# Alternating the four pages of an expert group row by row in DRAM

## What is computed

```python
def ffn(x, expert_sel, keys, values):          # 64 experts, 128 wide
    sel_val, sel_idx = top_k(sigmoid(x @ expert_sel.T), 4)
    gates = zeros.at[row, sel_idx].set(sel_val)
    h = einsum('nd,kde->nke', x, keys)
    return einsum('nke,kev->nv', relu(h) * gates[:, :, None], values)

x = x + attn_a(layernorm(x))   # causal, 16 heads of 8, rotary, W_attn, W_proj
x = x + ffn(layernorm(x), ...)
x = x + attn_b(layernorm(x))   # one head, local band of 64, softmax
x = x + ffn(layernorm(x), ...)
```

## Time and profile before

| | us |
|---|---|
| median of 3 runs | 1199.96 |
| lowest and highest run | 1194.97, 1205.8 |
| span of the profiled execution | 1216.6 |

### The profile page before, as it was taken

One profiled execution on the slowest core, in us unless ns is written; L12 is line 12 of the kernel. 1 busy time (PEld: TensorE's weight loads), 2 busy tenths in 40 slices (PEclk: granted clock), 3 DMA queues, 4 the chain that ended last, 5 costly groups with the idle time before them and its releaser, 6 DMA issues.

```text
span 1216.6 us, 22596 instructions
## 1 busy us (share of the span) xinstructions
PE 818.3 (67%) x7290; PEld 601.3 (49%) x7290; DVE 728.4 (60%) x2057; ACT 560.2 (46%) x1505; POOL 876.4 (72%) x934
## 2 busy tenths in 40 slices
PE   1899978888688766697898665454458874991000
PEld 0444444443344325697898644343357774991000
DVE  3787988888878424764667846566256772661111
ACT  1177666676566743564565413333126552661000
POOL 6345667879767675887888878878727578887776
PEclk9789999999999986898999866567679897996555
DMA  6556544533272332599898412212325564994222
GB/s 182 171 181 210 191 159 172 171 99 105 75 232 58 96 95 76 144 264 215 176 215 177 81 44 42 39 46 37 100 72 162 149 183 127 263 273 106 69 63 63
DMA packets 226258, 163.80 MB, mean 135 GB/s; under 512 B 15968, under 2 KB 213600, under 8 KB 226144
## 3 DMA queue, kind: packets, MB, share of 16 engines
q1 hardware_dynamic: 183968, 110.43, 31.7%
q0 software_dynamic: 36096, 33.59, 13.8%
q10 hardware_dynamic: 6080, 18.35, 4.1%
HBM read 78.94 MB, written 83.36 MB: 133 GB/s over the span
## 4 chain that ended last, share of the span: by engine, by line
PE 37%; POOL 23%; DVE 15%; issue 14%; ACT 6%; another core or an unknown queue 3%; DMA 3%; ACTq 0%; POOLq 0%; DVEq 0%; SPq 0%
POOL x_res L1743 7%; PE ps L771 6%; PE ps L780 5%; PE ps L672 5%; POOL sorted_rows L1727 4%; POOL v_aug L1745 3%; PE ps L631 3%; PE ps L760 3%; POOL x_scaled L1745 2%; ACT arena L978 2%; DMA x_res<-result_rows,dest 2%; DVE row_max L1211 2%; PE ps L689 2%; POOL arena L1776 1%
## 5 line engine op out<-in xcount | busy, mean ns | idle before, releaser
L1743 POOL DMA_INDIRECT x_res<-result_rows,dest x176 | 274.1, 1557 | 60.6 <-issue 48.8
L978 ACT ACTIVATE arena<-ps 128x512 f32<-128x512 f32 x320 | 182.8, 599 | 79.9 <-PE ps L604 75.1
L1727 POOL DMA_INDIRECT sorted_rows<-v_aug,dest x144 | 139.7, 970 | 83.7 <-issue 33.8
L1410 DVE COPY arena<-ps 128x512 f32<-128x512 f32 x128 | 88.2, 689 | 132.0 <-PE ps L760 71.7
L771 PE MATMUL ps<-arena 128*128 128x128 f32 x1024 | 147.2, 290 | 23.0 <-DVE arena L1410 11.5
L631 PE MATMUL ps<-arena 64*128 64x128 bf16 (+3 forms) x576 | 130.2, 305 | 28.9 <-DMA arena<-k_parts 15.1
L771 PEld LDWEIGHTS ps<-arena 128*128 128x128 f32 x1024 | 134.4, 205 | 26.9 <-issue 13.9
L1211 DVE TENSOR_REDUCE row_max<-ps 128x1 f32<-128x512 f32 (+1 forms) x192 | 127.0, 682 | 33.6 <-PE ps L651 31.9
L967 ACT COPY arena<-ps 128x512 f32<-128x512 f32 x128 | 75.0, 586 | 145.6 <-PE ps L780 117.0
L780 PE MATMUL ps<-arena 128*128 x1024 | 140.1, 281 | 0.9 <-ACT arena L967 0.9
L1727 POOL DMA_INDIRECT sorted_rows<-x_scaled,dest x112 | 111.5, 995 | 35.9 <-issue 24.6
(11 more groups left out here) (207 smaller groups left out, 1649.5 us busy)
## 6 DMA issues: line engine op xcount, KB each, us to landing
arena<-sorted_rows SPq DMA_DIRECT2D x128, 256.0 KB
result_rows<-arena SPq DMA_DIRECT2D x128, 256.0 KB
sorted_rows<-arena ACTq DMA_DIRECT2D x16, 1024.0 KB, 4.6
arena<-q_parts SPq DMA_DIRECT2D x16, 512.0 KB, 4.0
arena<-k_parts SPq DMA_DIRECT2D x16, 512.0 KB, 5.0
q_parts<-parts SPq DMA_DIRECT2D x52, 128.0 KB, 2.8
k_parts<-parts SPq DMA_DIRECT2D x38, 128.0 KB, 3.0
x_res<-result_rows,dest POOLq DMA_INDIRECT x176
```

The costliest lines, as they stand in the source:

```text
L978: nc.scalar.activation(prob[:, grp % 2, pr % 2, PROB_AT[u]:PROB_AT[u] + T], ps[:, v % 2, :], ACT.Exp, scale=SCALE_A).then_inc(exp_done, 1)
L1410: nc.vector.tensor_copy(xtt[:, n % 2, :], ps[:, e_bank(0, layer, half, n), :]).then_inc(t1_done, 1)
L1727: g.indirect_dma_start(sorted_d[b // HALF][:, :], bass.IndirectOffsetOnAxis(dest[:, 16 * b + n:16 * b + n + 1], 0), scaled_rows(layer, b)[ ...
L1743: g.indirect_dma_start(x[:, TT * b + t, :], None, rows, index, compute_op=ALU.add).then_inc(lane, 16)
```

## The change

In DRAM, the 512 rows of a group (four pages of 128) are laid out anew: row `r` of page `g` of the group stands at place 4 `r` + `g` instead of 128 `g` + `r`. A partition's four rows of a group, which stand side by side in `xin` and `yout`, are then side by side in DRAM as well, 2 KB. Both the load and the store read the tensor that way, and DVE works out from each row number the new one by shifts and masks: bits 7 and 8 go to bits 0 and 1, bits 0 to 6 move up by two, and the higher bits stay. `dest` serves the scatters and the gathers alike.

```diff
+        dest_i = sb("dest_i", [P, TT * TOPK], I32)
+        dest_page = sb("dest_page", [P, TT * TOPK], I32)
+        dest_row = sb("dest_row", [P, TT * TOPK], I32)
...
+        place_seq = sem("place_seq")
...
                         sp.dma_start(xin[:, G * (n % U):G * (n % U) + G, :],
-                                     sorted_d[half].rearrange("(n g p) c -> n p g c", g=G, p=P)[s]).then_inc(x_in[n % U], 16)
+                                     sorted_d[half].rearrange("(n p g) c -> n p g c", g=G, p=P)[s]).then_inc(x_in[n % U], 16)
...
-                        sp.dma_start(result_d[layer][half].rearrange("(n g p) c -> n p g c", g=G, p=P)[s - AHEAD],
+                        sp.dma_start(result_d[layer][half].rearrange("(n p g) c -> n p g c", g=G, p=P)[s - AHEAD],
                                      yout[:, G * (n % U):G * (n % U) + G, :]).then_inc(y_sent[n % U], 16)
...
                 dve.wait_ge(dest_seq, 2 * b + 1)
-                nc.vector.tensor_copy(dest[:, 16 * (b % B):16 * (b % B) + 16], destf[:, :]).then_inc(dest_seq, 1)
-                yield 0.7
+                nc.vector.tensor_copy(dest_i[:, :], destf[:, :]).then_inc(place_seq, 1)
+                dve.wait_ge(place_seq, 4 * b + 1)
+                nc.vector.tensor_scalar(dest_page[:, :], dest_i[:, :], 7, G - 1, ALU.logical_shift_right, ALU.bitwise_and).then_inc(place_seq, 1)
+                nc.vector.tensor_scalar(dest_row[:, :], dest_i[:, :], 2, G * (P - 1), ALU.logical_shift_left, ALU.bitwise_and).then_inc(place_seq, 1)
+                dve.wait_ge(place_seq, 4 * b + 2)
+                nc.vector.scalar_tensor_tensor(out=dest_page[:, :], in0=dest_i[:, :], scalar=-G * P, in1=dest_page[:, :],
+                                               op0=ALU.bitwise_and, op1=ALU.bitwise_or).then_inc(place_seq, 1)
+                dve.wait_ge(place_seq, 4 * b + 4)
+                nc.vector.tensor_tensor(dest[:, 16 * (b % B):16 * (b % B) + 16], dest_page[:, :], dest_row[:, :],
+                                        ALU.bitwise_or).then_inc(dest_seq, 1)
+                yield 0.9
```

## The result

Over 20 runs each, the changed kernel has a median of 1205.88 us (1199.88 to 1210.45) and the kernel before 1196.07 us (1189.97 to 1205.8). The ratio is 1.0073, with a 95% interval of 1.0055 to 1.0092: slower by 8.7 us, under the 1% that counts as a change here, but not nothing. (The two medians lie 9.8 us apart.

The account below looks back on a forecast made before the run. PE held 37% of the chain, POOL 23%, DVE 15%, transfers 3%; POOL alone set the final stretch. Shorter waits (-0.3, -3.0, -0.2, -1.0) and DVE's address work (+3.2, +1.6) summed to +0.3 us: 1200.3 us, range 1185 to 1212.

Parts of the forecast that it names:

- rival 2: The transfers were hidden anyway: no wait shortens, only DVE's +4.8 us is left, 1204.8 us; chance 0.17.
- The packets' price: SP's loads and stores: 90 ns per 2 KB against 112 for four 512 B, 46 us less per engine overall.
- (a): At 544.13 us, the first gather's wait for a store shortens: -0.3 us (bounds -1.1 and 0).
- (b): From 544 to 871 us, most of POOL's waits for landings go: -3.0 us (bounds -3.6 and 0).
- (d): From 1021 to 1112 us, POOL's waits for landings shorten: -1.0 us (bounds -1.7 and 0).
- (c): At 871.62 us, PE starts sooner after layer 1's first six loads: -0.2 us (bounds -1.1 and 0).
- (e): Before 511 us, DVE's address work in eight batches, half on the path: +3.2 us (0 to 6.4).
- (f): From 544 to 871 us, POOL's chain covers DVE's address work; without that cover 0.8 us each.
- (g): From 893 to 1021 us, DVE's address work in three batches: +1.6 us (bounds +0.8 and +2.4).
- Rival 1: After six loads at 871.62 us, unknown-queue stalls of DVE and ACT go: 15.1 us less, 1185 us; chance 0.17.
- Rival 3: 544 to 664 and 1021 to 1101 us: gathers wait longer for their turn, 18 us, total 1222 us; chance 0.08.
- Rival 4: The runs aren't joined: SP's packet count stays at 183968 and the time is 1204.8 us; chance 0.04.

Follow-up runs that it names:

- the kernel with the runs alone: Kernel before with only loads and stores read in 2 KB runs, row numbers and DVE work as before: 1198.65 us, ratio 1.0018.
- the one with the budget alone: Kernel before with only the slot budget after DVE's destination copy raised from 0.7 to 0.9: ratio 1.0004.
- layer 0 alone: Kernel before with five place-preserving DVE address instructions in layer 0's eight batches only, one copy otherwise: 1200.5 us, ratio 1.0051.
- layer 1 alone: Kernel before with five place-preserving DVE address instructions in layer 1's eight batches only, one copy in layer 0's: ratio 1.0018.

## Why the prediction was right or wrong

The measured time lies in the range, and the change is within 1%, to which 0.71 was given. The sum was wrong. It had +0.3 us, with bounds of -6.7 and +8.8, and +8.7 was measured, at the upper bound. The case that came is rival 2 (0.17, +4.8 us): the transfers were hidden anyway, and only DVE's work is left, with a larger price than it had there. That 1205.88 lies so near rival 2's 1204.8 is partly luck: the sum was put on a median of 1199.96 us from three runs, and over 20 runs it is 1196.07.

- **The packets' price** was mis-sized. With 7 ns for each of some 990 signal packets (an estimate, from the fixed part of the prediction's line), 63.4% of 80 x 16 us over the 16.38 MB in 2 KB pieces (7998) is 101 ns a piece, where the line through 512 B and 4 KB gave 90; four times 512 B, worked out in the same way from the earlier trace rows, are 115. That is an eighth less and not a fifth. Over the span it is 31.7% of 1216.6 less 29.3% of 1204.0, 33 us per engine where 46 were foreseen (26 between the kernel with the runs alone and the one with the budget alone). No effect of this on the time was found.
- **(a), (b), (d): -4.3 us for POOL's waits** is the step that failed. I took every landing wait over the issue time for the doing of the crowded engines. Against (a) to (d) together, -4.5 us, the kernel with the runs alone has +2.2 us (-1.7 to +6.0). POOL's waits in the traces, first of the kernel with the budget alone (512 B) from 536 to 691 us and from 1001 to 1092 us, then of the one with 2 KB runs alone, at the same places:

```profile
POOL x_res L1743 <- DMA x_res<-result_rows,dest: 6.3, 8, 1.6
POOL x_res L1743 <- DMA result_rows<-arena: 2.2, 1, 2.2
...
POOL x_res L1743 <- DMA x_res<-result_rows,dest: 7.7, 14, 1.8
```

```profile
POOL x_res L1743 <- DMA x_res<-result_rows,dest: 6.4, 9, 1.7
POOL x_res L1743 <- DMA result_rows<-arena: 2.3, 4, 1.4
...
POOL x_res L1743 <- DMA x_res<-result_rows,dest: 3.7, 6, 1.1
POOL x_res L1743 <- DMA result_rows<-arena: 1.6, 2, 0.9
```

  In the first stretch nothing moves. In the second, 7.7 us against 5.3 looks like a gain, but the kernel before has 3.5 in 6 there with 512 B, and the 48 adding gathers take 90.2 to 93.0 us in the kernels with 512 B pieces and 91.5 to 92.2 in the three with 2 KB. In the whole trace after, landings hold POOL's adding gathers for 10.7 us in 17 waits, where the forecast had some 5 for 9.7 in 15. The landings themselves say the same. From the start of an adding gather's instruction to the last event of its semaphore, the median over the last 48 gathers is 4.5 to 4.7 us in the three kernels with 2 KB pieces and 4.3 to 4.9 us in the eleven with 512 B, where three gathers take 5.5: only the slowest few of 48 hold POOL. An SP queue at 63% in place of 72% doesn't shorten them; what sets them is not shown. I had written this down as the second rival's argument, and gave it too little.
- **(c)**: from the six loads at 866.85 us to PE's first transpose at 869.66 it is 2.81 us after, 2.93 in the earlier trace rows: 0.1 gained where 0.2 was foreseen.
- **The price of the address work**, 0.8 us a batch, was right for most batches and even a little high (0.63 more than the copy). Three of layer 0's blocks cost 1.38 us more, one 1.02 and one 0.77, so 7.8 us in layer 0 where 6.4 was the most of (e). The longest copy of 0.654 us in the earlier trace rows was the sign. I took the median and put the long ones aside as rare, without asking where they stood: they stood in batches 1 to 3, in the stretch that counts.
- **(e)**, half of it on the path, is the second error, 2.9 us: 6.1 us (3.2 to 9.0) of 7.7 were measured for layer 0 alone, 0.8 of it, where +3.2 was taken. In the profile after, `dest_f`'s reduction is on the chain at six of layer 0's eight batches, and the address instructions themselves at four, the three long blocks among them. That DVE is idle 12% of that stretch doesn't mean that a delay is caught up: PE's weight loads of the score products wait for DVE's maxima there, from 150 to 511 us 36.9 us in 54 waits.
- **(f), (g)**: layer 1 alone lost 2.2 us (-1.2 to 5.4), close to the 1.6 of (g) and the 1.9 of the three blocks' extra. Eight blocks in full would be 5.0, so POOL's cover is likely but not proven by this interval. The working of (g) misread a row: the 4.69 us in the earlier trace rows are no slack of the middle batch but the time that POOL stood idle until DVE had written the last batch's destinations. POOL waited for the middle batch's too, 13.54 us at 959.67 in the trace before, so nothing covers it.
- **Moved rows, 0**: nothing else shows, 1.008 against 1.0072.
- **Rival 1** took the stalls of one execution for a property of the kernel. They are on no other chain here, with either run length. That they went was one of the signs by which I would be wrong; it says nothing about the change. **Rival 3** is out: adding gathers still take 1.54 us and 0.30 of issue, and the last 48 no longer. **Rival 4** is out by the packet count.

## To carry to other kernels

A freer DMA queue is worth only the waits that a lighter queue ends; a wait for a landing need not come from the fullest queue, and a run with the transfers changed alone tells whether it does. Small instructions on an engine that others wait for in turn cost nearly their whole time when they are added (0.8 of it here, on an engine idle for 12% of that stretch); taking one such instruction a batch away gained nothing that could be measured. After a change in how work is split into slots, look in the trace whether its order moved at all: one kernel here was meant to spread five instructions, and left them where they were. When an instruction's durations have a long maximum beside a short median, look up where the long ones stand before pricing five more of it there.

## What was not expected of the hardware

A DVE instruction of 128x16 takes 0.16 to 0.18 us alone and up to 0.80 us beside POOL's 128x512 `AFFINE_SELECT`s (read from where they stand, not tried), while a DMA share of 1.02 beside it, or one of POOL's indirect DMAs, does next to nothing to it. On a DMA engine one 2 KB piece takes 101 ns and four of 512 B 115, by the two windows above, an eighth less, which no part of this kernel could use.
